# Channel mixing of the low modes: quarter-array products, one weight load into the first pass's space, copies across

## The reference, cut to what matters

```python
# x: (32, 64, 128, 128) float32, weights1: (64, 64, 20, 20)
def compl_mul2d(x1, x2):                    # x1: modes of x, x2: weights
    x1n, x2n = _neg_freq(x1), _neg_freq(x2)  # mode (a, b) -> (-a, -b) mod 20
    t1 = jnp.einsum('bixy,ioxy->boxy', x1, x2 + x2n)
    t2 = jnp.einsum('bixy,ioxy->boxy', x1n, x2 - x2n)
    return 0.5 * (t1 + t2)
# dht_2d: Hartley transform over the plane, divided by its norm
# _L0: idht_2d(zeros with the 20x20 low modes = compl_mul2d(dht_2d(x)[.., :20, :20], weights1))
# _L1: sqrt(gx*gx + gy*gy + 1e-8), gx and gy the two 3x3 Sobel filters per plane
x = x + _L0(group_norm(x))     # groups of 2 planes
x = x + _L1(group_norm(x))
```

## Time and profile before

| | |
|---|---|
| three runs: median, lowest, highest | 2379.87, 2378.97, 2386.64 us |
| the profiled execution | 2381.43 us, its span 2379.4 us |
| mean granted clock of PE, share of full speed | 0.973 |
| busy: PE, PE's weight loads | 2216.2 us, 1625.6 us |
| busy: DVE, ACT, POOL | 1805.4 us, 1984.9 us, 1612.6 us |
| first pass, about | 0 to 713 us |
| mixing, about | 714 to 896 us |
| second pass | from there to the end |

### The profile page before, as it was taken

How to read it: one execution, slowest core, us unless ns; L and a number is a source line. 1 busy time by engine, 2 the same in 40 slices (tenths; PEclk the granted TensorE clock), 3 DMA queues, 4 the chain that set the end, 5 groups by cost and what they waited for, 6 DMA issues and landing times.

```text
span 2379.4 us, 61113 instructions
## 1 busy us (share of the span) xinstructions
PE 2216.2 (93%) x21212; PEld 1625.6 (68%) x21212; DVE 1805.4 (76%) x2714; ACT 1984.9 (83%) x3700; POOL 1612.6 (68%) x916
## 2 busy tenths in 40 slices
PE   5999999999992587999999999999999999999998
PEld 4777777777782575666666666666666666666665
DVE  4888888888867155887887887886787787787777
ACT  5888888888863326999999989988989989989988
POOL 4766666676643025777777777777777777777776
PEclk9999999999996787999999999999999999999999
DMA  7777777777736421666666665666666666666666
GB/s 206 203 200 205 200 198 207 198 201 197 207 95 138 100 56 54 186 182 182 186 178 193 180 187 170 192 178 183 190 178 184 188 178 182 190 177 189 190 189 186
DMA packets 808889, 421.41 MB, mean 177 GB/s; under 512 B 20912, under 2 KB 807344, under 8 KB 807472
## 3 DMA queue, kind: packets, MB, share of 16 engines
q1 hardware_dynamic: 808624, 417.86, 61.9%
HBM read 283.56 MB, written 134.22 MB: 176 GB/s over the span
## 4 chain that ended last, share of the span: by engine, by line
PE 42%; DMA 10%; SPq 4%; issue 3%; ACT 3%; DVE 1%; ACTq 0%; POOLq 0%; POOL 0%; DVEq 0%
PE g_ps L1009 30%; DMA out<-xbuf 9%; PE y_ps L1001 7%; PE v_ps L989 5%; SPq L188 2%; SPq L916 1%; PE v_ps L977 1%; ACT gx L1077 1%; DMA xbuf<-x 1%; DVE g_ps L1169 1%; ACT g_ps L1090 1%; ACT g_ps L1083 1%; ACT p_hi L1064 0%; DVE xbuf L1163 0%; ACT v_sb L1070 0%
## 5 line engine op out<-in xcount | busy, mean ns | idle before, releaser
L1009 PE MATMUL g_ps<-p_hi,stencil 128*128 128x512 f32 x2048 | 852.2, 416 | 6.3 <-DVE xbuf L1192 3.7
L950 POOL TENSOR_TENSOR p_lo<-pairs,p_hi 128x1032 fp32r<-128x1032 f32 x256 | 617.1, 2411 | 309.2 <-ACT p_hi L1064 309.2
L1009 PE MATMUL g_ps<-p_lo,stencil 128*128 128x512 f32 x2048 | 818.1, 399 | 0.0
L1009 PEld LDWEIGHTS g_ps<-p_hi,stencil 128*128 128x128 f32 x2048 | 387.1, 189 | 284.1 <-POOL p_lo L950 135.5
L945 POOL TENSOR_TENSOR pairs<-xbuf 128x1032 f32<-128x1032 f32 x256 | 488.3, 1907 | 53.1 <-POOL p_lo L950 30.3
L1192 DVE SCALAR_TENSOR_TENSOR xbuf<-xbuf,rows,g_ps 128x256 f32<-128x256 f32 x1024 | 434.1, 477 | 87.1 <-ACT g_ps L1090 70.3
L1169 DVE TENSOR_TENSOR g_ps<-gx,g_ps 128x512 f32<-128x512 f32 x512 | 348.4, 695 | 171.2 <-ACT g_ps L1083 164.6
L290 POOL TENSOR_TENSOR m_lo<-xbuf,m_hi 128x512 fp32r<-128x512 f32 x256 | 305.7, 1194 | 225.2 <-ACT m_hi L400 224.0
L1009 PEld LDWEIGHTS g_ps<-p_lo,stencil 128*128 128x128 f32 x2048 | 387.7, 189 | 81.6
L1090 ACT ACTIVATE g_ps<-g_ps,rows 128x256 f32<-128x256 f32 x1024 | 406.0, 446 | 41.8 <-DVE g_ps L1169 25.5
L481 DVE TENSOR_REDUCE rows<-square 128x1024 f32 (+1 forms) x256 | 311.1, 1215 | 116.1 <-ACT square L432 116.1
(11 more groups left out here) (120 smaller groups left out, 2412.6 us busy)
## 6 DMA issues: line engine op xcount, KB each, us to landing
xbuf<-x SPq DMA_DIRECT2D x256, 512.0 KB, 5.2
xbuf<-x SPq DMA_DIRECT2D x512, 256.0 KB, 3.2
out<-xbuf SPq DMA_DIRECT2D x512, 256.0 KB, 3.5
xbuf<-weights SPq DMA_DIRECT2D x8, 800.0 KB, 11.4
wmix<-weights SPq DMA_DIRECT2D x8, 800.0 KB, 13.9
second_sb<-second SPq DMA_DIRECT2D x1, 1230.0 KB, 8.4
mats_sb<-mats SPq DMA_DIRECT2D x1, 704.0 KB, 6.6
first_sb<-first SPq DMA_DIRECT2D x1, 32.0 KB, 5.6
```

Source lines behind the costliest of these rows:

```text
L950: nc.gpsimd.tensor_tensor(p_lo[:, r % 2, :, 0:W + 1], pairs[:, r % 2, :, 0:W + 1], p_hi[:, r % 2, :, 0:W + 1].bitcast(FP32), ALU.subtract) ...
L1009: mm = nc.tensor.matmul(g_ps[h][:, axis], stencil[:, m, :], p[:, r % 2, 4 * h:4 * h + 4, o:o + W], start=n == 0, stop=n == len(todo) - 1)
```

## The change

It touches the mixing, what stands just before and behind it, and where space lies:

- The weights are loaded once. `wmix` now has room for all 64 output channels and lies where the first pass has its buffers. SP issues the eight pieces from within the first pass, each as soon as the buffers under it are free. Piece 0 lies in unused space, piece 4 under the second-axis constants of which the last user is waited for.
- Partitions 64 to 127 of `wmix` are plain copies of partitions 0 to 63, not mirrored: pieces 0, 1 and 6 by ACT, 5 and 7 by DVE, 4, 2 and 3 by POOL.
- DVE builds `near` (difference and sum for half of the rows of modes) with two pairs of operations, ACT its negative, and POOL the last rows. Partitions stay as they are: 64 channels of one plane of a pair in each half.
- A product is now of 64 rows, 64 columns of weights and 32 moving columns, in one of the two diagonal quarters of the array. The 32 moving columns are 16 tiles for a mode and 16 for its mirrored mode. Two products add up to one pair. There are 14 groups. PE issues the product of group n in the first quarter and that of group n - 1 in the other in turn, one after the other.
- The rows' sums of a tile are added on PE within the next tile (four instructions behind chunk 5), and those of the last tile behind its second axis.
- The spreading takes four products instead of eight (one number for each pair of planes that form a group), so `rows` has half as many results.
- In the second pass six small clears replace the clear of all of `coef`, ACT no longer waits for it, and two pairs of operations in the lead-in change places.

```diff
+            def weights(n):                                    # first pass, SP
+                o = slice(n * WCH, (n + 1) * WCH)
+                sp.dma_start(wmix[0:C, o], w_i[:, o, :]).then_inc(w_in[n], 16)
+            weights(0)
+            sp.wait_ge(pe_second, TILES + 1)
+            weights(4)
+            sp.wait_ge(summed, TILES * HALVES + 2)
+            sp.wait_ge(fold_done, TILES * CHUNKS)
+            sp.wait_ge(pe_mirror, TILES * HALVES + 2)
+            weights(1)
+            weights(2)
+            sp.wait_ge(tile_done, TILES)
+            weights(3)
+            sp.wait_ge(pe_second, TILES + 2)
+            for n in range(5, PIECES):
+                weights(n)
...
+            def stats(i):                                      # first pass, PE
+                pe.wait_ge(tile_done, i + 1)
+                for a in range(2):
+                    mm = nc.tensor.matmul(stat_ps[:, a, i:i + 1], rows[:, a, i, :], mat("ones")[:, 0:1],
+                                          start=True, stop=True, skip_group_check=True)
+                mm.then_inc(stats_pe, 1)
...
+                    if k == 5 and not is_first(i):
+                        stats(i - 1)
...
-            for t in range(TILES):
-                if t == TILES - 1:
-                    pe.wait_ge(tile_done, TILES)
-                for a in range(2):
-                    mm = nc.tensor.matmul(t_ps[0][:, a, t:t + 1], rows[:, a, t, :], mat("ones")[:, 0:1],
-                                          start=True, stop=True, skip_group_check=True)
...
             for k in range(CHUNKS - 1):
                 second_axis(TILES - 1, 1, k)
+            stats(TILES - 1)
...
+            copy(4)                                            # mixing, POOL
+            copy(2)
             pool.wait_ge(scaled, 1)
             pool.wait_ge(act_scaled, 1)
-            part(nc.gpsimd, 1, 0).then_inc(parted_pool, 1)
+            for v, minus in ((0, False), (1, False), (2, True)):
+                ...
+                for dst, c, m in ((row9[:, v, :, 0:1].unsqueeze(2), ...), (row9[:, v, :, 1:].unsqueeze(2), ...),
+                                  (own_rows[:, v], c2, m2)):
+                    P.tensor_tensor(dst, x, y, op)
+            P.tensor_tensor(own, both, both, ALU.add).then_inc(parted_pool, 1)
+            copy(3)
...
+            def product(n, q, j, s):                           # mixing, PE
+                part = slice(C * q, C * (q + 1))
+                a, b = groups[n][j]
+                if s:
+                    a, b = -a % MODES, -b % MODES
+                x = operands(*groups[n][j])[part, 1 - s:3 - s]
+                return nc.tensor.matmul(mix_ps[n % BANKS][part, j], wmix[part, :, a * MODES + b], x,
+                                        start=s == 0, stop=s == 1, skip_group_check=True)
...
+            pe.wait_ge(parted_act, 1)
+            pe.wait_ge(doubled, PIECES - 3)
+            pe.wait_ge(pool_doubled, 3)
+            for n in range(GROUPS + 1):
+                if BANKS <= n < GROUPS:
+                    pe.wait_ge(act_out if n % 2 == 0 else dve_out, (n - BANKS) // 2 + 1)
+                for even, odd in itertools.zip_longest(items(n), items(n - 1)):
+                    if even:
+                        run(n, 0, even)
+                    if odd:
+                        mm = run(n - 1, 1, odd)
...
+            copy(0)                                            # mixing, ACT
             act.wait_ge(root_in, 1)
             nc.scalar.activation(root, arg, ACT.Sqrt, scale=4.0 * NPIX).then_inc(rooted, 1)
...
-            part(V, 0, 0)                                      # mixing, DVE
-            part(V, 0, 1)
-            part(V, 1, 1).then_inc(parted_dve, 1)
+            for v, op in ((0, ALU.subtract), (1, ALU.add)):
+                for c, m in halves()[:2]:
+                    cut = slice(0, NEAR)
+                    last = V.tensor_tensor(near[:, v, :, cut, c[1]], grid[:, :, c[0], c[1]][:, :, cut],
+                                           grid[:, :, m[0], m[1]][:, :, cut], op)
+                last.then_inc((differences, parted_dve)[v], 1)
+            for n in (5, 7):
+                dve.wait_ge(w_in[n], 16)
+                double(V.tensor_copy, n).then_inc(doubled, 1)
...
-            V.memset(coef[:], 0.0).then_inc(coef_zero, 1)      # second pass, DVE
-            dve.wait_ge(coef_zero, 1)
+            for js, ks in ((slice(0, n + 1), n), (0, slice(n + 1, NB)), (n, slice(0, n)),
+                           (slice(n + 1, NB), 0), (slice(n + 1, 2 * n), 2 * n), (2 * n, slice(n + 1, NB))):
+                V.memset(coef[:, js, :, ks], 0.0)
```

More of the change, by code:

```diff
@@ L159, in build @@
         x_in = [sem(f"p2_x_in{s}") for s in range(XSTEPS)]
+        w_in = [sem(f"w_in{n}") for n in range(PIECES)]
         def mat(name):
@@ new lines, in own_product, with items @@
+            def own_product(n, q, j):
+                part = slice(C * q, C * (q + 1))
+                a = (n - RECTS) * H
+                return nc.tensor.matmul(mix_ps[n % BANKS][part, H - 1 + j, 0], wmix[part, :, a * MODES + j * H],
+                                        own[part, :, n - RECTS, j], start=True, stop=True, skip_group_check=True)
+            def items(n):
+                if not 0 <= n < GROUPS:
+                    return []
+                pairs = [(j, s) for j in range(len(groups[n])) for s in range(2)]
+                return pairs + [(j, None) for j in range(2) if n >= RECTS]
@@ L682, in _ @@
             scaling.then_inc(act_scaled, 1)
-            for n in range(NW):
-                mirror_weights(n)
-            act.wait_ge(parted_dve, 1)
-            act.wait_ge(parted_pool, 1)
-            for n in range(0, 2 * GROUPS, 2):
-                if n == GROUPS + 1:
-                    act.wait_ge(mixed, GROUPS)
-                    for piece in range(NW, 2 * NW):
-                        mirror_weights(piece)
+            copy(1)
+            act.wait_ge(differences, 1)
+            nc.scalar.activation(near[:, 2].rearrange("p t a b -> p t (a b)"),
+                                 near[:, 0].rearrange("p t a b -> p t (a b)"), ACT.Copy, scale=-1.0)\
+                .then_inc(parted_act, 1)
@@ L693, in _ @@
+            copy(6)
+            todo = 0
+            for n in range(0, GROUPS, 2):
                 act.wait_ge(mixed, n + 1)
-                for dst, src in mixed_pieces(n):
+                for dst, src in evictions(n):
                     cp = nc.scalar.activation(dst, src, ACT.Copy)
                 cp.then_inc(act_out, 1)
-                for b in range(BATCHES):
-                    m, last = batch(b)
-                    if last // 2 * 2 != n:
-                        continue
-                    act.wait_ge(act_out, n // 2 + 1)
-                    act.wait_ge(dve_out, (last + 1) // 2)
-                    if b >= 2:
-                        act.wait_ge(reduced, b - 1)
-                    nc.scalar.activation(batch_view(0, b), modes[:, :, m], ACT.Square).then_inc(m_squared, 1)
+                while todo < len(batches) and (batches[todo][2] < n or n == GROUPS - 2):
+                    starts, rows_n, last = batches[todo]
+                    evicted(act, last)
+                    if todo:
+                        act.wait_ge(reduced, todo)
+                    for h, a in enumerate(starts):
+                        m = rows_n * MODES
+                        sq = nc.scalar.activation(squares[:, :, h * m:(h + 1) * m],
+                                                  modes[:, :, a * MODES:a * MODES + m], ACT.Square)
+                    sq.then_inc(m_squared, 1)
+                    todo += 1
@@ L767, in reduce_batch @@
                     .then_inc(reduced, 1)
+                for h, a in enumerate(starts):
+                    dve.wait_ge(m_late, 2 * b + h + 1)
+                    V.tensor_reduce(partial[:, 1, 2 * b + h, :], late[:, :, a * MODES:(a + n) * MODES],
+                                    axis=AX.X, op=ALU.add).then_inc(reduced_late, 1)
             todo = 0
-            for n in range(1, 2 * GROUPS, 2):
+            for n in range(1, GROUPS, 2):
                 dve.wait_ge(mixed, n + 1)
-                for dst, src in mixed_pieces(n):
+                for dst, src in evictions(n):
@@ L773, in _ @@
                     cp = V.tensor_copy(dst, src)
                 cp.then_inc(dve_out, 1)
[L776 removed]
+                if todo < len(batches) - 1 and n >= batches[todo][2] + 4:
                     reduce_batch(todo)
                     todo += 1
[L779 removed]
+            for b in range(todo, len(batches)):
                 reduce_batch(b)
[L781 removed]
+            dve.wait_ge(reduced, len(batches))
@@ L1122, in _ @@
             act.wait_ge(setup, 1)
-            for u in range(4):
+            for u in range(3):
                 copy_v(0, u)
             high(0, 0)
+            copy_v(0, 3)
             def step(i, r):
```

278 lines of the change are left out of this document (139 added, 139 removed).

## The result

The changed kernel takes 2359.76 us (median of 8 runs, 2354.20 to 2361.74) against 2379.42 us for the kernel before (8 runs, 2369.26 to 2386.64): ratio 0.9921, 95% interval 0.9901 to 0.9941. It is faster by 19.7 us, 0.8%. Forecast were 43. That the time lies next to rival 3's 2359 us is chance: rival 3 was a preparation that gets no shorter, and the preparation did get shorter. The profiled execution took 2360.06 us, span 2358.3; the kernel before had 2381.43 and 2379.4.

The account below looks back on a forecast made before the run. Two long stages bound near PE, with a gap between that the change works on. From 2381.4 us, 3.5 - 10.5 - 12.2 - 19.4 + 3.1 - 3.8 - 3.7 = -43.0 gave 2338.4 (2337 by the median); range 2286 to 2360.

Parts of the forecast that it names:

- rival 3: Preparation before the mixing gets no shorter, 53 us to the first product: +22, 2359 us in all; chance 0.08.
- The 256 steps don't change.: Second pass: its 256 steps were taken as unchanged, 0 us.
- The sum ahead of the second pass: All terms from the first pass to the start of the second pass added up: -43.0 us.
- First pass and its tail: Start to the mixing block: +3.5 us for added instructions in the tiles, -10.5 us for an earlier block start.
- The four statistics products of a tile: First pass on PE: four more instructions in each of 15 tiles, partly absorbed by waits, +3.5 us (0 to 7.5).
- The second axis: Last tile of the first pass: 172 loads at full clock take 5.1 us rather than 7.33.
- Preparation: Block start to first mixing product: 31 us instead of 43.2, -12.2 us (24 to 44).
- Mixing: First to last mixing product: 97.8 us instead of 117.2, -19.4 us, at 56 to 57 ns an instruction.
- Rival 1: Mixing: the quarters give the full gain, 29 ns an instruction, mixing 50 us, time 2289 us; chance 0.12.
- rival 2: Mixing: loads don't overlap, 110 ns an instruction, mixing 177 us, +79, 2416 us in all; chance 0.07.
- Behind the mixing: Last mixing product to DVE's second chain: DVE reduces the third batch only behind its last copy, +3.1 us.
- Spreading and clearing: Second chain to first transpose: four spreading steps drop out, -3.8 us; six small clears replace a large one, -3.7 us.

Follow-up runs that it names:

- e1: The changed kernel with nine already satisfied waits on SP ahead of the second pass's loop, which then begins at instruction 127 instead of 118: 2331.32 us.
- e17: The changed kernel with SP's second loop written as a nested loop, 342 instructions instead of 515, begun at the same place 118: 2332.6 us.
- e5: The changed kernel with each mixing product reading 64 adjacent weight words instead of words 400 apart: 2345.66 us.
- e7: The changed kernel with all mixing products of a step in the lower quarter first, then all in the upper, instead of in turn: 2428.11 us.
- e8: The changed kernel with nine satisfied waits ahead of SP's second loop, loads one step behind stores, and POOL's clearing of coef_t held back: 2323.58 us.
- e10: e9 with the mixing weights read from 64 adjacent words a partition: 2320.66 us.
- e9: e8 with 27 idle-time products of 512 columns on PE while it waits for the prepared operands: 2325.01 us.

## Why the prediction was wrong

- **"The 256 steps don't change."** This is the step that failed: 0 was forecast, +27.8 us measured. It was costed by what the change does to the second pass's instructions, which is nothing. The runs showed in its place that SP's loop, 515 instructions long, is fetched anew at each jump back in seven of nine places, not from 120 and 127, and that the change moved it from 127 to 118 (e1: all of it back with nine empty waits; e17: all of it back with a shorter body). Why these two places escape is open. It could have been suspected from the kernel before: its waits show SP's loads late in 53 of 256 steps, a hint at how little slack that queue had, though these waits cost nothing by themselves, and a changed length of SP's list was part of the diff. How much it would cost could not be read there, since no jump back in the second pass had a stall in it.
- **The sum ahead of the second pass was right,** -43.0 forecast, -48.9 measured, and e1 is the change without the accident: 2331.3 us where 2337 was forecast. Each stretch of the table holds within about 3 us.
- **First pass and its tail, -7.0, measured -9.4.** The four statistics products of a tile cost nearly nothing: the last tile's last chunk begins at 690.40 against 689.94, +0.5 for 60 instructions where +3.5 was taken. From there to the block start it is -9.8, where -10.5 was forecast. The second axis ran in 5.44 us (5.1 forecast) and at the full clock, as foreseen.
- **Preparation, 31 us, measured 29.7.** Mechanism as foreseen, DVE shut out while POOL works; the copies were oversized, POOL's at 4.4 us, measured 2.85, and DVE's at 3.5, measured 1.8 and 2.5. POOL's nine small operations last 13.5 us, but most of that is waiting for DVE: the last three, with DVE done, take 1.7 us, so nine by themselves would be about 5 (an estimate from these), near the 5.5 for POOL's share. DVE's 5120 elements of `near` are 5.6 us at the rate of L752, not 5.8, and measured 7.2 beside POOL. Rival 3 is out.
- **Mixing, 97.8 us, measured 94.8.** That the spread words set what a load costs, and that loads for different rows overlap, both stand: 110 ns alone was forecast as 111, and 55 in turn as 56 to 57. But the forecast did not see that the clock would stay at half, and in the changed kernel the array's own turn is then nearly as long as the supply, 106 against 110 ns. The number came out right because the spread words cost 110 ns at both clocks and because 106 is just under it; the second was luck. Rival 1 (29 ns) fails on the spread words, and by e5's 53.3 ns would fail on the clock too; rival 2 is what e7 made by hand, +71 us of mixing.
- **Behind the mixing +3.1, measured +2.5.** Spreading and clearing, together -7.5, measured -6.3: clearing gave less, since POOL's memset now falls on DVE's coefficients instead of on DVE's clearing (e8 takes that 4.1 us back).

## What to carry to other kernels

A change that adds or removes instructions ahead of a loop moves that loop in the engine's list; a long unrolled body can then be fetched at every jump back, as SP's was here (the same was not tried on other engines). Keep the body of a queue's loop short, 342 instructions against 515 here, and read the timeline of the queue at each jump back before believing that an untouched stage is untouched. And give a queue that stores and reloads slots a step of slack: don't let it wait for the store it has just issued.

## What was not expected of the hardware

- PE is busy 94.76 of 95 us by the profile in the mixing with two diagonal quarters, and the granted clock is 0.50 all the time. Where the clock was 1.0 when it began, it fell 2.3 and 3.3 us later (e10, e9).
- SP's gap at a jump back is 5.6 to 6.3 us from place 118, with three fetches, and 3.4 to 4.4 us from the six others, with two.
- A POOL copy of 3200 float32 elements takes 2.85 us, and 27 idle-time products on PE (26 us) slowed nothing beside them: the first mixing product stands 29.9 us behind the block start in e9 as in e8.
